# Retention layer: score products on 32-row parts of TensorE, queries masked for four heads at once, value bias added by GpSimd

## The chip, the cores and the metric

One core of one Trainium2 chip runs the program. The metric is the device time in microseconds (us). The kernel before takes 3194.3 us, the median of three runs (3193.05 to 3195.33). All numbers are float32.

## The reference, cut to what matters

The program is a chain of twelve layers on 2048 tokens of 128 features (2 batches of 1024). Only one layer is changed, the second, which the kernel calls `retention`. It gets the normalised x and its result is added to x:

```python
qkv = x @ W_qkv.T + b_qkv
q, k, v = jnp.split(qkv, 3, axis=-1)
# 16 heads of 8 features each
q = _apply_rope(q, cos, sin)
k = _apply_rope(k, cos, sin)
scores = jnp.einsum('bhtd,bhsd->bhts', q, k)
mask = jnp.tril(jnp.ones((length, length), dtype=x.dtype))
retention = scores * mask[None, None]
out = jnp.einsum('bhts,bhsd->bhtd', retention, v)
```

There is no softmax, so the product can be split: inside a tile of 128 tokens the masked scores are formed, and all earlier tiles enter through a running sum of k times v, the state.

## The kernel before, in words

Each layer is a block of its own with one program per engine; a barrier of all engines stands between two layers. In every block the order of the work on an engine is the order in which it is written, and semaphores tie the engines together. x, the weights and all intermediates stay in SBUF.

The retention block works on 16 tiles of 128 tokens, in 4 chunks of 4 tiles (`TPC` = 4). It has two parts.

The preparation goes chunk by chunk. TensorE turns the normalised rows (L268), ScalarE copies them to `xnT` (L1545), TensorE forms q and k and their rotated partners (L1458, L1460), then the values of four tiles (L1466), each with a second product of one row of ones by the bias row (L1468) into the same place, and turns the keys of the chunk before (L1444). VectorE applies the rotary tables (L1604, L1606, L1609) and the normalisation of the chunk ahead (L183, L186, L193). ScalarE copies the values and the turned keys out of PSUM (L1555, L1558). The tables come by four DMAs that SyncE issues at the start of the block (L1436); ScalarE and VectorE wait for all four.

The main loop goes in 16 waves, four per chunk. A wave is four heads on the four tiles of a chunk, so a wave has four steps, one for each tile. For a wave ScalarE makes four copies of the chunk's queries, each with all but one head's 8 features set to zero (`single_heads`, L1568). A step is one score product (L1482): 128 keys by 4 heads x 128 queries, contracted over all 128 features, of which the zeros leave 8. VectorE multiplies the 128x512 result by the triangle of ones (`mask`, L1616). Then four products (L1495) multiply the masked scores of each head by its 8 value columns; they go to four column groups of the array, 32 columns apart. TensorE issues step k+1's scores ahead of step k's values. Once per wave there is also one product of keys and values for the state (`outer`, L1504), which VectorE adds up (L1627 to L1632), and ScalarE copies the wave's values out of PSUM (L1580). After the first wave of each next chunk, TensorE puts the finished chunk together (`results`, L1517 and L1520: one product with the state and four that put the heads in place, for each tile), and VectorE adds it to x (L1638). In the waves 13 and 14 VectorE also does the first chunk's statistics and normalisation for the next layer.

PSUM has eight banks. The main loop gives the scores a ring of three, the state product one, the values two and the results two. A matmul in float32 appears in the trace as two weight loads and two matmuls, called two passes here.

Outside the block nothing is changed, except that the two constant tables `one_of` and `place` are filled in another way.

Of the kernel before, what the change touches and what calls it, by code (L numbers as in the profile page):

```python
# [25 lines left out]
P = 128  # L26
# [46 lines left out]
def macaron(nc, a, out):  # L73
    with ExitStack() as ctx:
# [1328 lines left out]
        def retention(tag, after):  # L1403
# [7 lines left out]
            qz = c(3 * GROUP * CHUNK).rearrange("p (n j t) -> p n j t", n=3, j=GROUP)  # L1411
            pr = c(8 * CHUNK).rearrange("p (n j t) -> p n j t", n=8, j=GROUP)
# [6 lines left out]
            HEADS = 4 * GROUP  # L1419
            one_of = c(HEADS + 1)  # L1420
            s = sems(tag, "tab stats rstd xn tp xT vec pool proj rope ktp ktc vps vcp qz st pm u sd "
                          "zero av oc y x")
            PER_BATCH = SEQ // P
            OUTER = 3
            OWN, SUM = (4, 5), (6, 7)

            STEPS = CHUNKS * GROUP * TPC
# [5 lines left out]
            def sync(sp):  # L1433
                for dst, name in ((tab, "r0_tab"), (blocks, "same"), (one_of, "one_of"),
                                  (place, "place")):
                    sp.dma_start(dst, a[name]).then_inc(s.tab, 16)  # L1436

            def tensor(pe):
# [10 lines left out]
                for ch in range(CHUNKS):  # L1449
# [24 lines left out]
                def own_scores(k):  # L1474

                    w, i = divmod(k, TPC)
                    n = w // GROUP * TPC + i
                    if i == 0:
                        pe.wait_ge(s.qz, w + 1)
                    if k >= 3:  # L1480
                        pe.wait_ge(s.pm, k - 2)
                    nc.tensor.matmul(ps[:, k % 3, :].rearrange("p (j t) -> p j t", j=GROUP),  # L1482
                                     kT[:, n * P:(n + 1) * P], qz[:, w % 3, :, i * P:(i + 1) * P],
                                     start=True, stop=True).then_inc(s.st, 1)

                def own_values(k):

                    w, i = divmod(k, TPC)
                    n, g = w // GROUP * TPC + i, w % GROUP
                    if i == 0 and w >= 2:  # L1490
                        pe.wait_ge(s.oc, w - 1)
                    pe.wait_ge(s.pm, k + 1)
                    for j in range(GROUP):
                        h = GROUP * g + j
                        last = nc.tensor.matmul(ps[32 * j:32 * j + 8, OWN[w % 2], i * P:(i + 1) * P],  # L1495
                                                vt[:, n, 8 * h:8 * h + 8], pr[:, k % 8, j, :],
                                                start=True, stop=True, tile_position=(0, 32 * j))
# [9 lines left out]
                def results(ch):  # L1507

                    pe.wait_ge(s.oc, GROUP * (ch + 1))
                    if ch >= 2:  # L1510
                        pe.wait_ge(s.x, ch - 1)
                    for n in range(ch * TPC, (ch + 1) * TPC):
                        at = ps[:, SUM[ch % 2], n % TPC * P:(n % TPC + 1) * P]
# [28 lines left out]
            def scalar(act):  # L1542
# [6 lines left out]
                act.wait_ge(s.tab, 64)  # L1549
# [11 lines left out]
                def single_heads(w):  # L1561
                    ch, g = divmod(w, GROUP)
                    act.wait_ge(s.rope, 2 * ch + 1)
                    if w >= 3:
                        act.wait_ge(s.st, TPC * (w - 2))
# [884 lines left out]
```

## Time and profile before

| | us |
|---|---|
| median of 3 runs | 3194.3 |
| the profiled execution | 3187.41 |
| its span, first to last instruction | 3185.7 |
| TensorE busy in the span | 2839.3 |
| VectorE busy | 2305.9 |
| ScalarE busy | 1871.4 |
| GpSimd busy | 511.1 |
| the retention block in the span | from about 221.1 to 380.8 |
| mean granted TensorE clock | 0.941 of full |

The profile is of one execution. Start times are us from the span's beginning. PE is TensorE's matmuls and PEld its weight loads, DVE is VectorE, ACT ScalarE, POOL GpSimd, SP SyncE. Matmuls are pipelined, so the time from one record's start to the next tells more than a record's own duration. A bracket at a row's end holds how long the engine was idle before it and what ended the wait.

### The profile page before, as it was taken

Reading aid. Unit: us, or ns where it says so; the run is one execution under the profiler, and the core shown is the slowest. Engines: PE = TensorE matmul, PEld = TensorE weight load, DVE = VectorE, ACT = ScalarE, POOL = GpSimd, SP = SyncE. Lnnn points to the kernel's source line nnn. Section 1 sums busy time; section 2 is a strip of 40 time slices with the busy share of each in tenths; the row PEclk is TensorE's granted clock in tenths of the full one; section 3 lists DMA queues with packets and bytes.
Section 4 is the critical chain, followed back from the end, with each engine's and each line's share of the span. In section 5 each row is a group of like instructions: output and inputs, shape, how many; then the busy total and the mean of one; then the engine's idle time right before and its main releaser. Section 6 shows DMA issues by size and latency. Waiting matters only on the chain. (4 is left out here: it accounts for less than half of the span.)

```text
span 3185.7 us, 43575 instructions
## 1 busy us (share of the span) xinstructions
PE 2839.3 (89%) x15916; PEld 1065.8 (33%) x15916; DVE 2305.9 (72%) x3016; ACT 1871.4 (59%) x3785; POOL 511.1 (16%) x832
## 2 busy tenths in 40 slices
PE   5999989799999998789977999999988799976778
PEld 2443434222222222533322222222226333344336
DVE  5464545799999996466657999999954766654972
ACT  2214322388888887446654888888875466654103
POOL 0000000200000000122222000000002222222740
PEclk9998999699999999989996999999999799988979
DMA  3210032300000000121113000000000311000000
GB/s 115 87 61 1 4 97 76 127 19 19 19 19 19 19 19 24 56 72 48 38 33 122 19 19 19 19 19 19 19 23 12 98 42 45 25 26 26 0 0 15
DMA packets 68129, 122.86 MB, mean 39 GB/s; under 512 B 16194, under 2 KB 43075, under 8 KB 64748
## 3 DMA queue, kind: packets, MB, share of 16 engines
q1 hardware_dynamic: 67916, 120.08, 11.6%
q8 instruction: 127, 2.08, 0.3%
q14 instruction: 86, 0.70, 0.1%
HBM read 96.56 MB, written 23.48 MB: 38 GB/s over the span
## 5 line engine op out<-in xcount | busy, mean ns | idle before, releaser
L1282 DVE TENSOR_REDUCE arena<-ps 128x1 f32<-128x1024 f32 (+7 forms) x1536 | 1572.6, 1064 | 235.8 <-PE ps L909 155.6
L1160 ACT ACTIVATE arena<-ps 128x512 f32<-128x512 f32 (+3 forms) x2816 | 1382.5, 573 | 410.1 <-PE ps L972 409.2
L903 PE MATMUL ps<-arena 61*128 61x512 bf16 (+4 forms) x2816 | 955.1, 384 | 65.5 <-DVE arena L1282 35.1
L972 PE MATMUL ps<-arena 64*128 64x512 bf16 (+4 forms) x2816 | 746.8, 372 | 56.0 <-ACT arena L1160 35.6
L929 PE MATMUL ps<-arena 128*32 128x512 f32 (+3 forms) x5632 | 713.6, 579 | 0.7 <-POOL arena L1241 0.3
L972 PEld LDWEIGHTS ps<-arena 64*128 64x128 bf16 (+1 forms) x2816 | 206.3, 95 | 767.2 <-ACT arena L1160 541.7
L903 PEld LDWEIGHTS ps<-arena 61*128 61x128 bf16 (+1 forms) x2816 | 259.5, 96 | 409.5 <-DVE arena L1282 354.9
L337 PE MATMUL ps<-xnT,moe_up 128*128 128x512 f32 x480 | 234.4, 614 | 0.0
L453 ACT ACTIVATE arena<-ps 128x512 f32<-128x512 f32 x120 | 71.4, 597 | 226.6 <-PE ps L337 226.6
L523 DVE TENSOR_TENSOR arena<-arena,ps 128x512 f32<-128x512 f32 x120 | 82.2, 686 | 160.8 <-ACT arena L453 129.8
L1210 POOL TENSOR_TENSOR arena<-arena,ones 16x128 bf16<-16x128 f32 x96 | 42.8, 446 | 844.1 <-ACT arena L1145 781.4
L929 PEld LDWEIGHTS ps<-arena 128*32 128x32 f32 x5632 | 111.3, 108 | 158.6 <-issue 135.4
L348 PE MATMUL ps<-arena,moe_dn 128*128 128x512 f32 x240 | 123.7, 607 | 17.4 <-DVE arena L533 15.2
L1241 POOL TENSOR_SCALAR_AFFINE_SELECT arena<-arena 128x512 f32<-128x512 f32 x128 | 81.2, 634 | 361.0 <-ACT arena L1160 359.2
L337 PEld LDWEIGHTS ps<-xnT,moe_up 128*128 128x128 f32 x480 | 92.7, 197 | 113.4 <-issue 109.0
L909 PE MATMUL ps<-maskb,identb 128*128 128x128 bf16 x512 | 115.4, 230 | 0.0
L253 POOL TENSOR_SCALAR var<-mv 128x4 f32<-128x4 f32 x40 | 9.6, 239 | 654.9 <-DVE mv L186 654.9
L2022 ACT ACTIVATE xnT<-ps,cols 128x512 f32<-128x512 f32 x8 | 6.2, 774 | 172.7 <-PE ps L268 172.7
L1342 DVE RECIPROCAL hid<-hid 128x512 f32<-128x512 f32 x16 | 53.5, 3346 | 52.5 <-DMA hid<-f_o 30.2
L1197 POOL TENSOR_TENSOR arena<-arena,ones 128x128 f32<-128x128 f32 (+1 forms) x48 | 22.5, 470 | 386.4 <-PE ps L929 386.4
L268 PE MATMUL ps<-ident,xn 128*128 128x128 f32 x208 | 36.6, 305 | 51.9 <-DVEq L203 27.0
L533 DVE TENSOR_TENSOR arena<-arena 128x512 f32<-128x512 f32 x120 | 80.9, 683 | 0.0
(226 smaller groups left out, 2640.3 us busy)
## 6 DMA issues: line engine op xcount, KB each, us to landing
arena<-m_w SPq DMA_DIRECT2D x32, 512.0 KB, 3.6
arena<-f_q SPq DMA_DIRECT2D x60, 144.0 KB
arena<-f_k SPq DMA_DIRECT2D x180, 48.0 KB
arena<-m_w SPq DMA_DIRECT2D x64, 128.0 KB, 3.7
arena<-in_w SPq DMA_DIRECT2D x4, 2048.0 KB
arena<-a_q SPq DMA_DIRECT2D x14, 576.0 KB
arena<-a_k SPq DMA_DIRECT2D x42, 192.0 KB
a_q<-arena SPq DMA_DIRECT2D x44, 96.0 KB, 2.0
```

Of the source, the lines that this page charges most:

```text
L337: nc.tensor.matmul(ps[:, FIRST_UP + tile % RING, :], moe_up[:, w:w + P], xnT[:, ch * CHUNK:(ch + 1) * CHUNK], start=True, stop=True)\
L348: nc.tensor.matmul(ps[:, Y_BANK, :], moe_dn[:, i * D:(i + 1) * D], hid[:, n % HID_RING, :], start=i == 0, stop=i == ALL_HID - 1)\
L453: nc.scalar.activation(sg[:, n % 3, :], ps[:, FIRST_UP + (2 * n) % RING, :], ACT.Silu).then_inc(s.silu, 1)
L523: nc.vector.tensor_tensor(hid[:, n % HID_RING, :], sg[:, n % 3, :], ps[:, FIRST_UP + (2 * n + 1) % RING, :], ALU.mult)\
L533: nc.vector.tensor_tensor(hid[:, n % HID_RING, :], hid[:, n % HID_RING, :], wb[:, 3 * p if last_pair else i, :], ALU.mult)\
L903: last = nc.tensor.matmul(at[:, k0 // CHUNK, 0:n], score_rows(Qop[par], j, slice(q0, q0 + P)), score_rows(Kop[par], j, slice(k0, k0 + n)), ...
L909: last = nc.tensor.matmul(at[:, (width - 1) // CHUNK, off:off + P], identb[:, :], maskb[:, 0, :], start=False, stop=True)
L929: last = nc.tensor.matmul(ps[32 * j:32 * j + 32, O_BANK, off:CHUNK], vx[vpar][:, kb, j, :], pr[:, (at % 2) * 4 + j, off:CHUNK], start=kb = ...
L972: nc.tensor.matmul(ps[:, ring_bank(item), off:CHUNK], shifted_rows(Kop[par], j, slice(kb * P, (kb + 1) * P)), shifted_rows(Qop[par], j, sl ...
L1160: nc.scalar.activation(pr[:, (at % 2) * 4 + j, off:CHUNK], ps[:, ring_bank(item), off:CHUNK], ACT.Exp).then_inc(s.ex, 1)
L1241: nc.gpsimd.affine_select(block, block, [[0, GROUP], [1, P]], ALU.is_ge, zero_fill, base=0, channel_multiplier=-1).then_inc(s.tri, 1)
L1282: nc.vector.tensor_reduce(mq[:, half, j * 4 + qb:j * 4 + qb + 1], src, AXX, ALU.max).then_inc(s.sread, 1)
```

## The change

- The heads are grouped in another way: a wave takes one head out of each group of 32 features (heads m, 4+m, 8+m, 12+m, where it took four neighbours).
- One ScalarE instruction per wave zeroes all but 8 of each 32 features, so that `qz` holds one 128x512 copy per wave instead of four; `one_of` shrinks from 17 to 5 columns.
- The score product of a head and a tile is contracted over the 32 features of its group alone: 16 products of 32 rows, 128 keys and 128 queries per wave, instead of 4 of 128 rows, 128 keys and 512 queries. They go to four banks, one per head. Heads 0 and 1 (row groups 0 and 32) are issued in turn over the four tiles, then heads 2 and 3.
- The order is by waves: all scores of wave w+1, then all values of wave w. A mask takes one head's four tiles; its count and its size stay.
- The results have one bank instead of two, the state product has bank 7.
- The bias products are gone. The bias row is sent to all 128 partitions by a fifth DMA at the block's start, and GpSimd adds it to the values in SBUF, one 128x512 addition per chunk.

```diff
-            qz = c(3 * GROUP * CHUNK).rearrange("p (n j t) -> p n j t", n=3, j=GROUP)
-            pr = c(8 * CHUNK).rearrange("p (n j t) -> p n j t", n=8, j=GROUP)
+            qz = c(3 * CHUNK).rearrange("p (n t) -> p n t", n=3)
+            pr = c(8 * CHUNK).rearrange("p (n i t) -> p n i t", n=8, i=TPC)
+            vbias = c(D)
...
-            OUTER = 3
-            OWN, SUM = (4, 5), (6, 7)
+            OWN, SUM, OUTER = (4, 5), 6, 7
+            WAVES = CHUNKS * GROUP
...
+                sp.dma_start(vbias, a["rows"][0:1, 9 * D:10 * D].to_broadcast([P, D])).then_inc(s.tab, 16)
...
-                        nc.tensor.matmul(at, xnT[:, ch * CHUNK + n * P:ch * CHUNK + (n + 1) * P],
-                                         wp[:, 2, :], start=True, stop=False)
-                        last = nc.tensor.matmul(at, ones[0:1, :], row(9), start=False, stop=True)
+                        last = nc.tensor.matmul(at, xnT[:, ch * CHUNK + n * P:ch * CHUNK + (n + 1) * P],
+                                                wp[:, 2, :], start=True, stop=True)
...
+                def own_scores(w, side):
+                    ch = w // GROUP
+                    if side == 0:
                         pe.wait_ge(s.qz, w + 1)
+                    if w:
+                        pe.wait_ge(s.pm, GROUP * (w - 1) + 2 * side + 2)
+                    for i in range(TPC):
+                        t = slice(ch * CHUNK + i * P, ch * CHUNK + (i + 1) * P)
+                        for j in (2 * side, 2 * side + 1):
+                            r = slice(32 * j, 32 * j + 32)
+                            last = nc.tensor.matmul(ps[:, j, i * P:(i + 1) * P], kT[r, t],
+                                                    qz[r, w % 3, i * P:(i + 1) * P],
+                                                    start=True, stop=True, tile_position=(32 * j, 0))
+                    last.then_inc(s.st, 1)
+                def own_values(w):
+                    ch, m = divmod(w, GROUP)
+                    if w >= 2:
                         pe.wait_ge(s.oc, w - 1)
+                    pe.wait_ge(s.pm, GROUP * (w + 1))
+                    for i in range(TPC):
+                        for j in range(GROUP):
+                            h = GROUP * j + m
+                            last = nc.tensor.matmul(ps[32 * j:32 * j + 8, OWN[w % 2], i * P:(i + 1) * P],
+                                                    vt[:, ch * TPC + i, 8 * h:8 * h + 8],
+                                                    pr[:, w % 2 * GROUP + j, i, :],
+                                                    start=True, stop=True, tile_position=(0, 32 * j))
                     last.then_inc(s.av, 1)
...
-                pe.wait_ge(s.vcp, CHUNKS)
+                pe.wait_ge(s.vb, CHUNKS)
...
-                own_scores(0)
+                own_scores(0, 0)
+                own_scores(0, 1)
                 pe.wait_ge(s.zero, 1)
-                for w in range(CHUNKS * GROUP):
+                for w in range(WAVES):
                     outer(w)
-                    for k in range(w * TPC, (w + 1) * TPC):
-                        if k + 1 < STEPS:
-                            own_scores(k + 1)
-                        own_values(k)
+                    if w + 1 < WAVES:
+                        own_scores(w + 1, 0)
+                        own_scores(w + 1, 1)
+                    own_values(w)
...
+                    nc.scalar.activation(qz[:, w % 3, :], qT[:, ch * CHUNK:(ch + 1) * CHUNK], ACT.Identity,
+                                         bias=one_of[:, GROUP:GROUP + 1],
+                                         scale=one_of[:, m:m + 1]).then_inc(s.qz, 1)
...
+                for ch in range(CHUNKS):
+                    tiles = vt[:, ch * TPC:(ch + 1) * TPC, :]
+                    pool.wait_ge(s.vcp, ch + 1)
+                    nc.gpsimd.tensor_tensor(tiles, tiles, vbias.unsqueeze(1).to_broadcast([P, TPC, D]),
+                                            ALU.add).then_inc(s.vb, 1)
```

## Rows read from the trace of the kernel before

**Rows 1.** Windows: preparation, main loop; wall, busy of each engine (records), clock, DMA.
```profile
218.00:265.60 47.60, 37.69 (x133) 21.13 (x132) 24.91 (x62) 10.14 (x18) 3.78 (x6) 0.85 0.09 30
265.60:380.80 115.20, 112.60 (x824) 48.13 (x824) 55.62 (x106) 51.64 (x76) 1.26 (x2) 0.97 0.00 1
```

**Rows 2.** Timeline of a wave: start us, us, engine, line, operation.
```profile
275.02 0.30 PEld L1504 LDWEIGHTS ps<-arena 128*128 128x128 f32 x2 [0.22 <-issue]
...
276.63 0.30 PEld L1482 LDWEIGHTS ps<-arena 128*128 128x128 f32 x2 [0.22 <-issue]
...
277.69 0.12 PEld L1495 LDWEIGHTS ps<-arena 128*8 128x8 f32 x8 [0.76 <-DVE arena L1616]
...
278.02 0.30 PEld L1482 LDWEIGHTS ps<-arena 128*128 128x128 f32 x2 [0.22 <-issue]
...
280.81 0.30 PEld L1504 LDWEIGHTS ps<-arena 128*128 128x128 f32 x2 [0.22 <-issue]
```

**Rows 3.** Timeline, the results of chunk 0.
```profile
298.17 0.97 PEld L1520 LDWEIGHTS ps<-arena 128*128 128x128 f32 x8 [0.22 <-issue]
...
301.29 0.30 PEld L1517 LDWEIGHTS ps<-arena 128*128 128x128 f32 x2
...
302.41 0.30 PEld L1504 LDWEIGHTS ps<-arena 128*128 128x128 f32 x2
```

**Rows 4.** Timeline, values and bias of chunk 1, then the turned keys of chunk 0.
```profile
235.66 0.19 PEld L1466 LDWEIGHTS ps<-wproj,xnT 128*128 128x128 f32 x1 [0.24 <-issue]
...
238.05 0.30 PEld L1466 LDWEIGHTS ps<-wproj,xnT 128*128 128x128 f32 x2
...
238.88 0.42 PEld L1444 LDWEIGHTS ps<-ident,arena 128*128 128x128 f32 x4
```

**Rows 5.** Timeline of layer f1: 64-row and 61-row products; float32 loads in 32-column groups.
```profile
900.34 0.16 PEld L929 LDWEIGHTS ps<-arena 128*32 128x32 f32 x8 [0.23 <-issue]
...
901.34 0.39 PE L972 MATMUL ps<-arena 64*128 64x512 bf16 x1
901.35 0.39 PE L903 MATMUL ps<-arena 61*128 61x512 bf16 x1
901.57 0.38 PE L972 MATMUL ps<-arena 64*128 64x512 bf16 x2
```

**Rows 6.** Timeline, VectorE: the block's start, and late in the loop.
```profile
227.01 0.75 DVE L1604 SCALAR_TENSOR_TENSOR arena<-ps,cols,arena 128x512 f32<-128x512 f32 x1 [1.76 <-DMA arena<-in_place]
...
233.44 0.42 PEld L268 LDWEIGHTS ps<-ident,xn 128*128 128x128 f32 x4 [0.70 <-DVE xn L193]
...
363.37 0.68 DVE L1638 TENSOR_TENSOR x<-x,ps 128x512 f32<-128x512 f32 x1
...
365.66 1.28 DVE L1616 TENSOR_TENSOR arena<-ps,masks 128x512 f32<-128x512 f32 x2
```

**Rows 7.** Timeline: chunk 3's last rotation, the first queries, the loop's first and last instructions.
```profile
258.39 0.69 DVE L1609 TENSOR_TENSOR arena<-arena 128x512 f32<-128x512 f32 x1
...
262.57 2.92 ACT L1568 ACTIVATE arena<-arena 128x512 f32<-128x512 f32 x4
...
265.60 0.50 PEld L1482 LDWEIGHTS ps<-arena 128*128 128x128 f32 x2 [3.96 <-issue]
...
375.32 0.30 PEld L1517 LDWEIGHTS ps<-arena 128*128 128x128 f32 x2 [1.00 <-ACT arena L1580]
```

**Rows 8.** Groups: durations (min/median/max ns), first and last start.
```profile
L1632 DVE TENSOR_TENSOR arena<-arena x12: 291/292/293, 275.9 to 365.4; 128x128 f32<-128x128 f32 x12
L1192 POOL TENSOR_TENSOR arena<-arena x32: 1147/1153/1173, 578.5 to 2526.7; 128x512 bf16<-128x512 f32 x32
```

**Rows 9.** Windows, columns as in Rows 1: the clock beside the bias products, and early in the loop.
```profile
229.00:240.00 11.00, 10.54 (x46) 6.38 (x44) 9.55 (x26) 1.02 (x2) 1.27 (x2) 1.00 0.01 2
266.00:270.00 4.00, 4.00 (x14) 1.33 (x13) 1.03 (x3) 4.00 (x7) 0.00 (x0) 0.50 0.01 4
```

**Rows 10.** Timeline, twelve small products in the first layer.
```profile
58.71 0.91 PE L375 MATMUL ps<-ident,arena 9*128 9x9 f32 x12
```

More of the change, by code:

```diff
@@ L1472, in tensor @@
                 turn_keys(CHUNKS - 1)
[L1474 to L1478, printed above, removed]
+                def own_scores(w, side):
+                    ch = w // GROUP
+                    if side == 0:
                         pe.wait_ge(s.qz, w + 1)
[L1480 to L1490, printed above, removed]
-                        pe.wait_ge(s.oc, w - 1)
[L1492 to L1497, printed above, removed]
+                    if w:
+                        pe.wait_ge(s.pm, GROUP * (w - 1) + 2 * side + 2)
@@ L1509, in results @@
                     pe.wait_ge(s.oc, GROUP * (ch + 1))
[L1510 to L1511 removed]
+                    if ch:
+                        pe.wait_ge(s.x, ch)
                     for n in range(ch * TPC, (ch + 1) * TPC):
[L1513 removed]
+                        at = ps[:, SUM, n % TPC * P:(n % TPC + 1) * P]
                         first = n % PER_BATCH == 0
@@ L1559, in scalar, with quarter @@
                                          ACT.Copy).then_inc(s.ktc, 1)
-                def single_heads(w):
-                    ch, g = divmod(w, GROUP)
+                def quarter(w):
+                    ch, m = divmod(w, GROUP)
                     act.wait_ge(s.rope, 2 * ch + 1)
                     if w >= 3:
-                        act.wait_ge(s.st, TPC * (w - 2))
-                    for j in range(GROUP):
-                        h = GROUP * g + j
-                        last = nc.scalar.activation(qz[:, w % 3, j, :],
-                                                    qT[:, ch * CHUNK:(ch + 1) * CHUNK], ACT.Identity,
-                                                    bias=one_of[:, HEADS:HEADS + 1],
-                                                    scale=one_of[:, h:h + 1])
-                    last.then_inc(s.qz, 1)
+                        act.wait_ge(s.st, 2 * (w - 2))
+                    nc.scalar.activation(qz[:, w % 3, :], qT[:, ch * CHUNK:(ch + 1) * CHUNK], ACT.Identity,
+                                         bias=one_of[:, GROUP:GROUP + 1],
+                                         scale=one_of[:, m:m + 1]).then_inc(s.qz, 1)
                 for w in range(3):
-                    single_heads(w)
+                    quarter(w)
                 for w in range(CHUNKS * GROUP):
-                    act.wait_ge(s.av, TPC * (w + 1))
+                    act.wait_ge(s.av, w + 1)
                     if w >= 2 * GROUP:
@@ L1581, in scalar @@
                         .then_inc(s.oc, 1)
-                    if w + 3 < CHUNKS * GROUP:
-                        single_heads(w + 3)
+                    if w + 3 < WAVES:
+                        quarter(w + 3)
             def gpsimd(pool):
@@ L1610, in vector, with mask @@
                             .then_inc(s.rope, 1)
-                def mask(k):
-                    dve.wait_ge(s.st, k + 1)
-                    if k >= 8:
-                        dve.wait_ge(s.av, k - 7)
+                def mask(w, j):
+                    dve.wait_ge(s.st, 2 * w + j // 2 + 1)
+                    if w >= 2 and j == 0:
+                        dve.wait_ge(s.av, w - 1)
                     nc.vector.tensor_tensor(
-                        pr[:, k % 8], ps[:, k % 3, :].rearrange("p (j t) -> p j t", j=GROUP),
-                        masks[:, 2, :].unsqueeze(1).to_broadcast([P, GROUP, P]), ALU.mult)\
+                        pr[:, w % 2 * GROUP + j], ps[:, j, :].rearrange("p (i t) -> p i t", i=TPC),
+                        masks[:, 2, :].unsqueeze(1).to_broadcast([P, TPC, P]), ALU.mult)\
                         .then_inc(s.pm, 1)
@@ L1642, in vector @@
                 nc.vector.memset(ps[:, OWN[0]:OWN[1] + 1, :], 0.0).then_inc(s.zero, 1)
-                mask(0)
-                for w in range(CHUNKS * GROUP):
+                for j in range(GROUP):
+                    mask(0, j)
+                for w in range(WAVES):
                     next_state(w)
-                    for k in range(w * TPC, (w + 1) * TPC):
-                        if k + 1 < STEPS:
-                            mask(k + 1)
+                    if w + 1 < WAVES:
+                        for j in range(GROUP):
+                            mask(w + 1, j)
                     if w % GROUP == 1 and w > 1:
```

16 lines of the change are left out of this document (7 added, 9 removed).

## The prediction

> **What bounds the kernel now.** The layers are cut apart by barriers, so I read only the retention block, first by windows. In the main loop (265.6 to 380.8) TensorE is busy 112.6 of 115.2 us, VectorE 55.6, ScalarE 51.6 [rows 1]. So TensorE sets the pace. The timeline says with what. One step runs from 276.63 to 278.02, 1.39 us [rows 2]. From the scores' first load to the values' first load it is 1.06 us (277.69 - 276.63), then 0.33 us of values. In dense products of the same type a tile of ten passes over 128 columns takes 1.12 us (302.41 - 301.29), 0.11 us a pass [rows 3], so 512 columns are about 0.43 us a pass and the two passes of a score product 0.85. The rest of 1.06, some 0.2 us, is a first load that nothing hides, and the emptying of the array before the shape of its parts changes; the same stands in the 0.33, as two passes of 128 columns are 0.22 and the four column groups run side by side. A wave takes 5.79 us (275.02 to 280.81), of which 5.79 - 4 x 1.39 = 0.23 is the state product [rows 2].
>
> The preparation (to 265.6) is a chain of TensorE, ScalarE and back [rows 4], with two places where VectorE or a DMA comes last [rows 6].
>
> **The main loop, part by part.** Scores: 16 products a wave, 32 passes of 128 columns, as many columns as before. What can go is the half of them that lies beside the other half. No row shows 32-row products in float32. The nearest are the 64- and 61-row products of layer f1, in bfloat16: a pair on different row groups starts within 0.01 us, and the next starts 0.22 us later [rows 5], so two products take the time of one. That float32 loads of several parts overlap too is seen in column groups: eight loads of 32 columns take 0.16 us, where two of 128, as many columns, take 0.30 [rows 2, 5]. Bounds: full overlap, 16 passes of 0.11 = 1.78 us; none, 3.56 us. I take full overlap. With a first load (0.11) and one emptying (0.1): 2.0 us.
>
> The page "TensorE: Matmul & The Clock Gate" of the Trainium skill (LDWEIGHTS) says that a load's time goes by its columns, not its rows, and (The mechanism) that a load passes a running matmul only on another row group. By this each part would alternate load and product, and two parts would give 3.5 us a wave instead of 1.8. In this trace loads on the same rows do hide: 0.11 us a pass with a new 128-column load each [rows 3].
>
> Values: 16 products a wave in four column groups, so 8 passes of 0.11 = 0.89, plus 0.1 of emptying: 1.0 us (4 x 0.33 = 1.32 before) [rows 2]. State product: it now stands between two changes of shape. Exactly this is in the bias stretch, where value products of two passes take turns with one-row products: one of each takes 0.83 us (238.88 - 238.05), 0.41 apiece [rows 4]. Sum: 0.41 + 2.0 + 1.0 = 3.4 us a wave instead of 5.79, 2.4 us less.
>
> Does VectorE keep up? Four masks back to back are 4 x 0.62 (two in 1.28 us, [rows 6]) and the state 0.29 for each of its two instructions plus a small gap [rows 8]: 3.1 us, under 3.4. Worked through in order from the start of the state product: S0 (heads 0, 1) ends at 1.4, masks from 1.5 to 4.0; S1 of the next wave starts at 3.4 + 1.4 = 4.8 and needs the last mask, 0.8 us of slack; the next state update ends at 4.7, when the next masks may start (4.9). So TensorE still leads, with 0.2 us to spare. ScalarE, busy 51.6 us of the loop before [rows 1], loses three of four query masks, so it stays hidden. The single results bank waits for an addition three waves old, hidden.
>
> At the end it isn't hidden: in wave 13 the addition (0.68) and the statistics (in all from 363.37 to the masks at 365.66, with a state update of 0.6 in it) [rows 6] stand ahead of wave 15's masks, so 1.7 us plus a wait for them. With 3.1 of 3.4 us used, wave 15's values come 2.4 us late.
>
> Loop: before, 375.32 - 265.60 = 109.7 us to the last results [rows 7]. After: first scores 1.9; half clock at the start as before (0.50 in 266 to 270, [rows 9]; with its edges I take 5.5 us of TensorE work at half speed), 2.8; 15 waves of 3.4 = 51; three in-loop results as before, 4.24 each (302.41 - 298.17, [rows 3]) = 12.7; last values 1.0; the late masks 2.4; ScalarE's copy 0.8. Sum 72.6, so **37 us less**. The last results are unchanged.
>
> **The preparation.** Values of a chunk take 238.88 - 235.66 = 3.22 us, eight turns of 0.41 [rows 4]; without the bias products 8 passes of 0.11 and one first load, 1.0 us: 2.2 us less for each chunk. What follows hangs on it (the turned keys, L1444 [rows 4], their copy L1558, the copy L1545, then the next projection). Chunk 0's gain is lost: TensorE next waits for VectorE's normalised rows at 233.44, whose chain starts at 227.01 when the last table lands [rows 6]. That chain starts later, too: the fifth DMA is issued behind the fourth, which I put at +0.45. Bounds: 0, if it lands with the others, and 1.8, the wait for the fourth once more [rows 6]; the value taken is nearer to the first, as transfers in flight overlap. Chunks 1 and 2 give 4.4. In chunk 3 the values gain 2.2, but turning the last keys needs VectorE's last rotation, which ends at 258.39 + 0.69 = 259.08, some 6 us ahead of the loop [rows 7]. Between it and the loop stand the last turned keys, their copy and the query mask, so a part of the 2.2 is lost behind it; the older chunk's keys are turned first and fill the wait. I count 1.9, with 0 and 2.2 as its bounds. The first queries: four instructions of 2.92 us in all become one of 0.80, 2.2 less [rows 7]. GpSimd's last addition is near 1.15 us (the L1192 row, same size, [rows 8]) behind the value copy; key turning, key copy and query mask behind the same copy take longer (the mask alone is 2.92 / 4 = 0.73, [rows 7], and a key copy of the same size stands before it), so it hides. Were it 3 us it would cost 1. Sum 4.4 + 1.9 + 2.2 - 0.45 = **8 us less**.
>
> Total 45 us. The profiled execution took 3187.4, 6.9 us below the median of the runs; taken from the median, 3194.3 - 45 = **3149.3 us**.
>
> **Rivals.**
>
> A: the score parts don't overlap, because the 128-column loads go one after another or because float32 pairs run in turn. For: no float32 row groups in the trace. Against: both halves of it appear separately [rows 5]. A wave is 0.41 + 3.8 + 1.0 = 5.2 us, 0.6 less; VectorE has room again, so no late end: 16 x 0.6 = 9, plus 8 from the preparation: 17 to 19 us less, 3176.
>
> B, slower: TensorE can't be fed. A wave has 132 loads and matmuls. At 3.4 us this is 51 ns for each pair of load and matmul; before, 42 pairs in 5.79 us, 138 ns. The densest longer run of pairs that I find is of twelve in 0.91 us, at most 76 ns each [rows 10], and they may have been queued ahead; over a longer stretch none is denser than the results' 111 ns [rows 3]. At 76 ns a wave is 66 x 0.076 = 5.0 us, 26 us of the gain gone: 3175. Half of that is 3162. At 111 ns it is 7.3: the loop 1.5 x 16 = 24 us longer, less 8, so 3210. It decides above (5.79 + 0.5)/66 = 95 ns. Against: the eight loads of the values all lie within 0.12 us [rows 2]. The same page of the Trainium skill (section "Wait — 56ns, not 53.3ns?") gives some 62 ns for each matmul where it is decoded in software: by it alone a wave would be 66 x 0.062 = 4.1 us, an estimate, and the time 3160.
>
> C, slower: the granted clock stays at half (1.2 GHz) in the loop, as half the rows work. Passes double: a wave 6.5, results 8.5: so the loop is 16 x 0.7 + 4 x 4.3 = 28 us longer, less 8: 3214. Against: in the bias stretch, half of whose products had one row, the clock was 1.00 [rows 9]. It was at half in the loop's first us, behind 3.96 us without a load [rows 7, 9], and this pause gets shorter.
>
> D: VectorE leads because masks slow down beside TensorE's writes to four banks or beside GpSimd. At 3.8 us a wave: 3156. This is a shade of the forecast.
>
> **How the numbers follow.** Forecast with D and a small part of B: 0.72, own range 3141 to 3163. A, or B up to 76 ns: 0.17. B beyond 95 ns: 0.05. C: 0.03. The rest, 0.03, ends near no change. A measurement of this kernel can tell 0.2%, 6.4 us, from none. Faster 0.89, same 0.03, slower 0.08. The range reaches from 3140 (all passes overlap, clock drops vanish) to 3178 so as to hold A.
>
> **What would show it.** Right: in the changed trace two score matmuls on different row groups start together, the time between state products is 3.3 to 3.6 us with TensorE without gaps; masks come in fours, 0.62 us apart; the preparation is some 8 us shorter; the last masks are late behind the statistics. Wrong: score matmuls 0.11 us apart one by one (A), gaps between loads while all waits are met (B), 0.50 in the clock column (C), TensorE idle before scores until a mask (D).

## The result, and the profile after

| | before | after |
|---|---|---|
| median, us | 3193.68 (4 runs, 3189.15 to 3195.33) | 3140.53 (4 runs, 3137.83 to 3144.41) |
| ratio, 95% interval | | 0.9839, 0.9824 to 0.9854 |
| the profiled execution / its span | 3187.41 / 3185.7 | 3137.83 / 3136.1 |
| retention block, barrier to barrier | 160.5 | 114.1 |
| the other eleven layers together | 3025.2 | 3022.0 |

The kernel is 53 us faster; the forecast was 45 less. The measured 3140.5 lies at the lower edge of what was forecast: 0.5 us under the range of 3141 to 3163 that had the chance of 0.72, and 0.5 above the lower end of the whole range, 3140 to 3178. In the profiled executions 46.4 us of the 49.6 come from the changed block. The other 3 come from layers in which no work changed. There the clock stood at half for 355 us before and for 338 after; over all the kernels below the sum over these layers went from 3016.2 us, with 331 at half clock, to 3030.8, with 372. These stretches fall otherwise in every execution. So the block's own length, barrier to barrier, is the sharper measure, and I use it beside the medians.

The block has three parts. From its first instruction to the loop's first score load: 265.60 - 221.34 = 44.26 before, 251.53 - 219.42 = 32.11 after, 12.1 less (forecast 8). From there to the last results: 109.7 before, 324.16 - 251.53 = 72.6 after, 37.1 less (forecast 37). The last results, to the end of the last addition: 5.5 before, 331.80 + 0.69 - 324.16 = 8.3 after, 2.9 more (forecast: nothing).

Windows of the kernel after: the preparation, the loop's first stretch, the middle of the loop, the stretch behind the last values (columns as in [rows 1]).

```profile
218.00:251.50 33.50, 24.19 (x96) 13.54 (x96) 24.67 (x62) 7.40 (x14) 8.85 (x10) 0.95 0.13 44
251.70:265.20 13.50, 13.50 (x160) 11.28 (x164) 8.02 (x15) 2.43 (x4) 0.00 (x0) 0.50 0.00 1
265.60:298.00 32.40, 32.14 (x570) 28.74 (x568) 21.42 (x42) 10.39 (x16) 0.00 (x0) 1.00 0.01 2
323.40:330.20 6.80, 6.09 (x32) 6.04 (x29) 0.00 (x0) 0.60 (x1) 0.00 (x0) 0.50 0.01 2
```

In the middle TensorE is busy 32.14 of 32.40 us at the full clock: it leads, as forecast. But the loop's first 13.5 us and the block's last results stand at 0.50, and busy is 13.50 of 13.50: no window of busy time would show that this half is lost.

The timeline of one wave after, which answers to [rows 2]:

```profile
271.79 0.49 PE L1507 MATMUL ps<-arena 128*128 128x128 f32 x2
272.21 1.53 PEld L1483 LDWEIGHTS ps<-arena 32*128 32x128 f32 x32
273.42 1.89 DVE L1621 TENSOR_TENSOR arena<-ps,masks 128x512 f32<-128x512 f32 x3 [0.18 <-PE ps L1483]
273.86 0.77 PEld L1497 LDWEIGHTS ps<-arena 128*8 128x8 f32 x32
274.85 0.52 PEld L1523 LDWEIGHTS ps<-arena 128*128 128x128 f32 x4 [0.22 <-issue]
```

State product 272.21 - 271.79 = 0.42 us, scores 273.86 - 272.21 = 1.65, values 274.85 - 273.86 = 0.99: 3.06 us for a wave of 66 load and matmul pairs, 46 ns a pair. VectorE waits 0.18 us for the scores. In a wave with an addition of results VectorE's work is longer, and it is VectorE that leads: the scores took 305.15 - 303.05 = 2.10, the wave 306.14 - 302.63 = 3.51.

```profile
302.63 0.49 PE L1507 MATMUL ps<-arena 128*128 128x128 f32 x2
303.05 1.99 PEld L1483 LDWEIGHTS ps<-arena 32*128 32x128 f32 x32
305.15 0.77 PEld L1497 LDWEIGHTS ps<-arena 128*8 128x8 f32 x32
306.14 0.30 PEld L1507 LDWEIGHTS ps<-arena 128*128 128x128 f32 x2 [0.22 <-issue]
```

The starts of single records in the first of these two waves show how 32 passes fit into 1.65 us, where 16 pairs of passes one after another, 0.11 each, would make 1.76 and a first load more:

```
row groups  0, 32: first passes start 272.212, 272.218; the next pair 0.21 later, then one every 0.11; last 273.095, 273.102
row groups 64, 96: first passes start 272.772, 272.779; the next pair 0.21 later, then one every 0.11; last 273.656, 273.662
```

The records don't name their row group; they are told apart by these steps. So the second pair of row groups, later in the program's order, began 0.32 us before the first pair had started its last pass, and for that time all four row groups work side by side.

The loop's start and end, TensorE's records:

```profile
251.56 3.00 PE L1483 MATMUL ps<-arena 32*128 32x128 f32 x32 [1.48 <-ACT arena L1570]
254.50 0.80 PE L1507 MATMUL ps<-arena 128*128 128x128 f32 x2
260.08 0.80 PE L1507 MATMUL ps<-arena 128*128 128x128 f32 x2
265.55 0.49 PE L1507 MATMUL ps<-arena 128*128 128x128 f32 x2
...
322.39 1.06 PE L1497 MATMUL ps<-arena 128*8 128x128 f32 x32 [2.63 <-DVE arena L1621]
324.16 0.50 PEld L1520 LDWEIGHTS ps<-arena 128*128 128x128 f32 x2 [1.00 <-ACT arena L1580]
...
331.80 0.69 DVE L1643 TENSOR_TENSOR x<-x,ps 128x512 f32<-128x512 f32 x1 [8.53 <-PE ps L1523]
```

Waves 0 and 1 take 5.58 and 5.47 us, not 3.06. At the end wave 15's values wait 2.63 us for the last mask.

### The profile page after: what moved, and what is told of

It is laid out like the page before. It is cut to its first block and busy times, and to the rows that moved or that the text cites. A ratio compares the mean times of both kernels' runs of the same rounds, so it can differ in the third digit from the quotient of the medians.

```text
span 3136.1 us, 44146 instructions
## 1 busy us (share of the span) xinstructions
PE 2777.3 (89%) x16220; PEld 1074.6 (34%) x16268; DVE 2302.1 (73%) x3016; ACT 1838.0 (59%) x3737; POOL 516.5 (16%) x836
## 5 line engine op out<-in xcount | busy, mean ns | idle before, releaser
L972 PE MATMUL ps<-arena 64*128 64x512 bf16 (+4 forms) x2768 | 735.0, 371 | 67.1 <-ACT arena L1160 39.8
```

The lines of the kernel that those rows point to most:

```text
L972: nc.tensor.matmul(ps[:, ring_bank(item), off:CHUNK], shifted_rows(Kop[par], j, slice(kb * P, (kb + 1) * P)), shifted_rows(Qop[par], j, sl ...
```

## The experiments

All kernels but one are the changed kernel with the tables `one_of` and `place` sent as in the kernel before and put in their new order by GpSimd on the chip. The first run is this control. Behind "Measured" stand the median, then its ratio to the kernel before, which ran beside it on the same chip. The block times, and the "half clock", which are the stretches of 0.50 in TensorE's clock column inside the block, are of the one profiled execution.

**Control.**

```diff
-    o["one_of"] = (feat[:, None] % 32 // hd == np.arange(GROUP + 1)[None, :])
+    o["one_of"] = (feat[:, None] // hd == np.arange(17)[None, :])
...
+                nc.gpsimd.tensor_tensor(one_of, pairs[:, 0:GROUP], pairs[:, GROUP:2 * GROUP], ALU.add)
```

> The changed kernel, with the two constant tables sent as before and put in the new order by GpSimd in the preparation (two additions of 16 and 8 columns, four copies of 128x128). It is the base of the experiments that follow. GpSimd idles there until the first value copy, so every theory expects the changed kernel's time: a median within 3 us of 3140.5, a wave of 3.1 to 3.2 us, and a retention block of 114 us.

Measured: 3141.44, ratio 0.9853 (0.9837 to 0.9869); block 114.4 us; half clock 3.41 us at 222.16, 13.65 from 252.88 and 6.83 from 324.56. It stands for the changed kernel.

**What the row groups are worth: the same order, all 128 rows in each product.**

```diff
-  nc.tensor.matmul(ps[:, j, i * P:(i + 1) * P], kT[r, t], qz[r, ...], tile_position=(32 * j, 0))
+  nc.tensor.matmul(ps[:, j, i * P:(i + 1) * P], kT[:, t], qz[:, ...])
```

> Each score product is contracted over all 128 rows instead of its 32, so it sums over the four heads of the wave and the output is another one; the number of products, their columns, the order by waves and all waits stay. It takes away the overlap alone. Theory (overlap): 32 passes of 0.11 in a row, scores 3.5 us, state product 0.21 (no change of shape behind it), values 1.0 and 0.1 for one change of shape: a wave of 4.9 us, 16 x 1.7 = 27 us slower than the base, 3167; so of the loop's gain of 2.6 us a wave, 1.7 is the overlap and 0.9 the order by waves. Rival (the order by waves is all): the wave stays at 3.1 and the time with it. Rival (narrow products cost clock): the half-clock stretch at the loop's start, 13.65 us in the changed kernel and 10.24 before, gets shorter.

Measured: 3164.74, ratio 0.9927 (0.9912 to 0.9942); block 133.9. Timeline of a wave, and a window over 10 us early in the loop:

```profile
268.98 0.49 PE L1510 MATMUL ps<-arena 128*128 128x128 f32 x2
269.20 3.65 PEld L1486 LDWEIGHTS ps<-arena 128*128 128x128 f32 x32
272.97 0.77 PEld L1500 LDWEIGHTS ps<-arena 128*8 128x8 f32 x32
273.96 0.30 PEld L1510 LDWEIGHTS ps<-arena 128*128 128x128 f32 x2 [0.22 <-issue]
...
257.50:267.70 10.20, 10.20 (x115) 9.86 (x115) 7.23 (x13) 1.30 (x2) 0.00 (x0) 1.00 0.01 2
```

The scores take 3.77 us, the wave 4.98. So the row groups bring 4.98 - 3.06 = 1.9 us a wave, and the new order alone 5.79 - 4.98 = 0.8. I put the 0.8 down to fewer changes of shape and fewer uncovered first loads; no run takes these apart. Rival A of the prediction had 3.8 us of scores and a wave of 5.2 without overlap; it is 3.77 and 4.98. The expectation's last rival holds as well: the half clock at the loop's start is gone, and so is that at the end. This is why the block lost only 133.9 - 114.4 = 19.5 us against the control and not 16 x 1.9 = 30: TensorE worked 6.8 us at half clock here and 23.2 in the control (8.2 us of time), and there is no wait of 2.6 us for the last masks.

**Does the overlap need the groups issued in turn?**

```diff
-                    for i in range(TPC):
-                        for j in (2 * side, 2 * side + 1):
+                    for j in (2 * side, 2 * side + 1):
+                        for i in range(TPC):
```

> The same 16 score products per wave, but one row group's four tiles one after another, then the next group's. Theory (the gain is the overlap of row groups, and it hangs on the order of issue, because TensorE looks only a few records ahead): products on one row group can't overlap, and the next group starts at most some three passes early, as the second pair did in the changed kernel (272.77, when the first pair had 0.33 us left). Scores 4 x 0.86 - 3 x 0.33 = 2.5 us instead of 1.65, a wave of 3.9 (3.5 to 4.3), 12 us slower than the base (6 to 18). Rival (the order is free, TensorE's window holds all of a wave): no change. Rival (the gain is the order by waves, with fewer changes of the array's shape): no change.

Measured: 3166.38, ratio 0.9931 (0.9916 to 0.9945); block 139.8. TensorE's timeline of a wave at the full clock, then two windows at half and one at full clock:

```profile
306.62 2.82 PE L1486 MATMUL ps<-arena 32*128 32x128 f32 x32
309.37 1.06 PE L1500 MATMUL ps<-arena 128*8 128x128 f32 x32
...
262.00:278.00 16.00, 16.00 (x142) 13.58 (x141) 6.47 (x13) 2.59 (x4) 0.00 (x0) 0.50 0.00 1
278.00:298.00 20.00, 20.00 (x181) 16.59 (x181) 8.76 (x16) 3.62 (x6) 0.00 (x0) 0.50 0.00 1
299.00:320.00 21.00, 21.00 (x307) 19.29 (x306) 11.89 (x22) 5.19 (x8) 0.00 (x0) 1.00 0.01 3
```

The scores take 2.75 us: TensorE does begin a later row group early, but only near the end of the earlier one (the records show the next group's first pass 0.33 us before the last of the group before). The overlap takes 3.77 - 2.75 = 1.0 us off a wave's scores, where pairs take 2.1 off. And the clock stays at half for 41 us, with TensorE busy without a gap in the windows shown, then goes to full in the same kind of work. So the kernel is 25 us slower than the control, where 6 to 18 were expected: the overlap's part was seen rightly, the clock's wasn't.

**All four row groups in turn.** One wait, for all masks of the wave before, ahead of all 16 products.

```diff
-                        for j in (2 * side, 2 * side + 1):
+                        for j in range(GROUP):
```

> All four row groups are issued in turn, as one group of 16 products that waits for all four masks of the wave before. Theory (all four row groups can run beside each other, and VectorE's four masks and the state update, 3.1 us, now set the wave): scores take 0.11 + 8 x 0.107 = 0.97 us instead of 1.65, but the time is worse, since VectorE now idles from its last mask to the end of the next scores: 2.48 of masks + 1.1 to 1.2 of scores and hand-over = 3.6 to 3.7 us a wave instead of 3.1 to 3.2, 8 us slower than the base. Rival (only two row groups run beside each other): scores stay at 1.65 or more, a wave of 4.2 us or more, 16 us slower. Rival (TensorE sets the wave and four groups make it shorter): a wave of 2.5, 9 us faster.

Measured: 3145.74, ratio 0.9868 (0.9851 to 0.9884); block 118.5. Timeline of a wave:

```profile
268.44 1.01 PEld L1488 LDWEIGHTS ps<-arena 32*128 32x128 f32 x32 [0.60 <-issue]
269.58 0.77 PEld L1502 LDWEIGHTS ps<-arena 128*8 128x8 f32 x32
269.71 2.48 DVE L1639 TENSOR_TENSOR arena<-ps,masks 128x512 f32<-128x512 f32 x4 [0.85 <-PE ps L1488]
272.31 0.34 PEld L1488 LDWEIGHTS ps<-arena 32*128 32x128 f32 x8 [1.44 <-ACT arena L1578]
272.34 0.39 PE L1488 MATMUL ps<-arena 32*128 32x128 f32 x4 [1.28 <-DVE arena L1639]
```

Scores in 1.14 us: four groups overlap too. But now nothing of a wave's masks lies beside its scores, TensorE idles 1.28 us for the last mask, and the wave takes 272.31 - 268.44 = 3.87: VectorE's 3.1 us of work and its wait of 0.85 for the scores stand one behind the other. Pairs are the better order. The block is 4.1 us longer than the control's; 8 were expected. The page "TensorEngine Tiling (Array Packing)" of the Trainium skill (PSUM Bottleneck) says that emptying PSUM may become the bottleneck once tiling makes TensorE faster; by the row above, it has: 2.48 us of masks and 0.6 of state updates to 2.55 us of TensorE's work.

**The value bias alone**, on the kernel before: fifth DMA, bias products out, GpSimd's addition in.

> The kernel before with one part of the change alone: no bias products, the bias row by a fifth DMA, added by GpSimd. Theory of the prediction's sum: 2.2 us less for chunks 1 and 2, 1.9 for chunk 3, 0.1 more for the fifth DMA: 6.2 us less at the same clock. The two half-clock stretches of the preparation (3.4 us each, at 240.7 and 251.0 in the kernel before) were absent in the changed kernel; if this part alone removes them it gives another 3 us, 9 in all. Rival (the preparation's gain was clock alone, and TensorE would have waited anyway): 3 us or less.

Measured: 3178.61, ratio 0.9955 (0.9938 to 0.9972); block 151.2, 9.3 less than before. TensorE's timeline: of the kernel before, behind the bias stretches, then the same places of this kernel.

```profile
238.47 0.48 PE L1468 MATMUL ps<-rows,ones 1*128 1x128 f32 x2
240.71 2.08 PE L1458 MATMUL ps<-xnT,wproj 128*128 128x512 f32 x2 [1.17 <-ACT xnT L1545]
...
251.43 2.08 PE L1458 MATMUL ps<-xnT,wproj 128*128 128x512 f32 x2 [1.18 <-ACT xnT L1545]
```

```profile
233.23 1.11 PE L268 MATMUL ps<-ident,xn 128*128 128x128 f32 x4 [2.20 <-DVE xn L193]
...
237.11 1.05 PE L1468 MATMUL ps<-wproj,xnT 128*128 128x128 f32 x8
239.77 1.12 PE L1460 MATMUL ps<-xnT,wproj 128*128 128x512 f32 x2 [1.18 <-ACT xnT L1546]
...
246.42 1.12 PE L1460 MATMUL ps<-xnT,wproj 128*128 128x512 f32 x2 [1.18 <-ACT xnT L1546]
...
257.20:260.50 3.30, 3.30 (x6) 1.10 (x4) 0.89 (x2) 3.30 (x6) 0.00 (x0) 0.50 0.00 0
```

Two passes of 512 columns take 1.12 us here and 2.08 before, behind a wait of 1.18 in both. Ahead of the wait, half of the value products had one row before; without them that stretch is also shorter, and no run takes the two apart. The half clock isn't gone from this kernel, though. A stretch of 3.41 us came at 233.23, behind a wait of 2.20 between products of 128 rows, and the one at the loop's start lasted 3.41 instead of 10.24. TensorE worked 16.4 us at half clock before and 10.2 here. That is 3.1 us of time, so 6.2 of the 9.3 are left at the same clock, the figure of the prediction's sum.

**The next layer's statistics behind the last masks.**

```diff
-                    if w == CHUNKS * GROUP - 3:
-                        ahead_stats(dve, s, t, CHUNKS, after)
-                    if w == CHUNKS * GROUP - 2:
-                        ahead_apply(dve, s, CHUNKS, after)
+                ahead_stats(dve, s, t, CHUNKS, after)
+                ahead_apply(dve, s, CHUNKS, after)
                 add(CHUNKS - 1)
```

> The base e0 with the next layer's statistics and normalisation moved behind VectorE's last masks, where VectorE idles 8.5 us. Theory (they hold up wave 15's masks: TensorE idles 2.6 us before the last values and the clock then falls for the last results, 2.9 us): block 5.5 us shorter, 3136. Without the clock's part 2.6. Rival (they hide, the last wave is late for another reason): no change.

Measured: 3139.96, ratio 0.9833 (0.9818 to 0.9847); block 111.8, 2.6 less than the control, where 5.5 were expected. TensorE's wait for the last mask fell from 2.63 to 1.46 us; that is this edit's doing. The half clock at the end fell from 6.83 to 3.41, but a stretch of 6.83 came at 333.59, in the next layer, which took 188.1 us where it had taken 185.5. This second part can't be put down to the edit: the control's own repeat, the last run below, has the same 3.41 at the end, another 6.83 in the next layer, and 188.0 us for it. The whole kernel gained nothing that can be told.

```profile
321.30 1.06 PE L1500 MATMUL ps<-arena 128*8 128x128 f32 x32 [1.46 <-DVE arena L1637]
```

**Two masks of 1024 columns instead of four of 512.**

```diff
-                        pr[:, w % 2 * GROUP + j], ps[:, j, :].rearrange("p (i t) -> p i t", i=TPC),
+                        pr[:, at:at + 2].rearrange("p n i t -> p (n i) t"),
+                        ps[:, 2 * side:2 * side + 2, :].rearrange("p j (i t) -> p (j i) t", i=TPC),
```

> The base e0 with the wide masks alone. If VectorE sets the wave where it has more than its four masks and the state update to do, the waves with an addition get shorter (3.1 to 3.2 instead of 3.2 to 3.5) and wave 15's values come 0.3 us earlier: 1 to 2 us in the block, 112 to 113 instead of 114.4. The half-clock stretch of 13.65 us at the loop's start stays, as the pause stays. Rival (masks don't matter): 114.4. Rival (a mask of two banks waits longer for its scores and delays the chain): 115 or more.

Measured: 3142.44, ratio 0.9846 (0.9829 to 0.9864); block 112.1, 2.3 less than the control. The pair takes 2.36 us where four take 2.48. Of the 2.3 us, 1.7 are a half-clock stretch of 3.41 instead of 6.83 at the end, which the control's repeat has as well (block 112.8). So 0.6 to 0.7 us may be the masks' own; by medians nothing is gained.

```profile
270.00 2.36 DVE L1638 TENSOR_TENSOR arena<-ps,masks 128x1024 f32<-128x1024 f32 x2 [0.18 <-PE ps L1486]
```

**What sets the clock at the loop's start?** In the kernel after, TensorE pauses 1.48 us (1.68 without a load) ahead of the first scores and then does 32-row products. Either could be the cause. One kernel keeps the pause and gives waves 0 and 1 all 128 rows:

```diff
+                            if w < 2:
+                                last = nc.tensor.matmul(ps[:, j, i * P:(i + 1) * P], kT[:, t],
+                                                        qz[:, w % 3, i * P:(i + 1) * P], ...)
+                                continue
```

> The base e0, but the score products of waves 0 and 1 are contracted over all 128 rows, as in the third experiment, so their output is another one; the pause before the loop stays. Theory N (narrow products let the clock stay at half after a pause; with all rows it had no half-clock stretch in the loop): no half-clock stretch at the loop's start, or one of 3.4 us at most. Theory P (the pause alone makes it, and the third experiment was luck): a stretch of 10 us or more as in the base. The two waves cost 1.9 us more each at full clock.

Measured in one execution: 3140.17; block 112.3. TensorE's timeline and the window:

```profile
254.69 3.81 PE L1487 MATMUL ps<-arena 128*128 128x128 f32 x32 [1.48 <-ACT arena L1581]
263.63 1.72 PE L1491 MATMUL ps<-arena 32*128 32x128 f32 x32
...
251.00:264.00 13.00, 10.29 (x113) 9.38 (x113) 7.99 (x14) 4.44 (x8) 1.26 (x1) 1.00 0.01 1
```

The pause is there, the half clock isn't, and the narrow products that follow run at full clock. Two waves of twice the passes cost no more than the half clock did.

The other kernel keeps the narrow products and takes the pause away: scores of wave 0 ahead of the last turned keys, query masks as soon as a chunk's queries are there; it has the late statistics as well.

```diff
-                turn_keys(CHUNKS - 1)
...
                 own_scores(0, 0)
+                pe.wait_ge(s.rope, 2 * CHUNKS)
                 own_scores(0, 1)
+                turn_keys(CHUNKS - 1)
```

> The kernel of the seventh experiment without the wide masks: early first scores and the late normalisation, four 128x512 masks a wave. If the pause before the loop is one of two conditions of the half clock there (the other being narrow products), the loop has no half-clock stretch, as in the seventh, and the block takes 102 + 2 = 104 us. If the seventh experiment's full clock was luck or came from the masks, the stretch of 10 to 14 us is back and the block takes 109 or more.

Measured: 3140.05, ratio 0.9837 (0.9817 to 0.9857); block 104.6. Timeline and window at the loop's start:

```profile
251.90 2.46 PE L1485 MATMUL ps<-arena 32*128 32x128 f32 x32
255.63 0.49 PE L1509 MATMUL ps<-arena 128*128 128x128 f32 x2 [0.69 <-ACT arena L1579]
258.80 0.49 PE L1509 MATMUL ps<-arena 128*128 128x128 f32 x2
...
250.00:262.00 12.00, 11.17 (x183) 9.24 (x182) 11.11 (x20) 2.98 (x5) 1.27 (x1) 1.00 0.00 1
```

Wave 0 takes 3.17 us at once. So the half clock at the loop's start goes with both together: a pause of 1.48 us and then narrow products. With both it came in all seven profiled executions that have them: for 13.65 us in four (after, the control, the late statistics alone, the wide masks alone), for 10.24 in two (the control's repeat, and the four row groups in turn, where it began only in a second pause of 2.27), for 41 in the one with the groups one after another. With the pause and 128 rows it came in neither of two (the third experiment's way and this section's first kernel), with narrow products and no such pause in none of three (this kernel and the last one, twice). The block gained 9.8 us over the control, or 7.2 over the kernel with the late statistics alone, yet the medians are level. In its profile the other layers took 3030.8 us, with 372 at half clock; the control's 3019.9, with 335. Whether that is this kernel's doing or chance, one profile of each can't say.

**All three together**, and again with five executions, beside the control on the same chip.

> e5 with two more edits: the first scores are issued ahead of the last turned keys, their query masks made by ScalarE while it idles in the preparation, so that TensorE idles no more than some 0.5 us there; and VectorE masks two heads' scores with one 128x1024 instruction, two a wave instead of four. Early scores: 1.5 to 2 us, and, if the half-clock stretch of 13.65 us at the loop's start comes from the pause before it, 5 us more; if it comes from the narrow products, nothing more. Wide masks: VectorE's 3.1 us a wave fall by 2 x 0.09 to 2.9, under TensorE's 3.06, worth 0.1 to 0.2 a wave in the waves with an addition and at the end, 1 to 2 us in all. Sum: 3 to 4 us under e5 with the half clock, 8 to 9 without.

Measured: 3130.55 (3119.93 to 3136.82), ratio 0.9802 (0.9779 to 0.9825); block 102.0, 2.6 less than without the wide masks. Of these 1.7 are a half-clock stretch of 3.41 us at 233.72 that only the other has.

> The kernel of e7_wide_masks again (early first scores, wide masks, late normalisation), with the base beside it on one chip. Its retention block took 102.0 us and the base's 114.4, while the other layers of single executions differ by up to 15 us in sum. If the block's gain is real in the whole kernel's time, the median is 9 to 13 us under the base's; if the other layers give it back, under 5.

Measured: 3131.21 (3127.38 to 3149.87), ratio 0.9819 (0.9794 to 0.9844); block 102.1; half clock only 3.41 us at 220.41.

> The base e0 again, beside the last kernel on one chip: 3137 to 3145 us, a retention block of 114 us with a half-clock stretch of 10 to 14 us at the loop's start, if that stretch belongs to the kernel and not to one execution.

Measured: 3139.78 (3138.34 to 3143.24), ratio 0.9838 (0.9824 to 0.9851); block 112.8; half clock 3.41 at 223.88 and 234.12, 10.24 at 254.60, 3.41 at 326.28.

The three together have the shortest block: 10.7 to 12.4 us under the control's. The medians are 8.6 us under it on one chip, just short of the 9 to 13 expected if the whole gain stays, and 10.9 in the first pair, which ran on two chips. The intervals of the last two ratios still overlap a little (0.9844 and 0.9824), so from the repeat alone the order of the two isn't proven; with the block times it is the likelier reading. In the first of the two profiles, the window over the end of the loop and the last results shows the clock at full throughout (the next half-clock stretch, 6.83 us, comes at 323.47 in the next layer):

```profile
300.00:320.50 20.50, 17.71 (x284) 15.93 (x280) 11.61 (x24) 3.09 (x5) 1.26 (x2) 1.00 0.01 2
```

## Why the prediction was right, and where only by luck

The steps of the block, by kernels: before 160.5; bias to GpSimd 151.2; order by waves and one query mask a wave 133.9; row groups 114.4; pause, late statistics and wide masks 102.0.

**The loop**: forecast 72.6 us, measured 72.6. The sum is right, its terms are not, and that it comes out is luck: the first scores and the waves were put 5.4 us too high, the half clock, the results, the last wait and the waves that VectorE leads 5.4 too low.

| term | forecast | measured |
|---|---|---|
| first scores, at full clock | 1.9 | 1.65 |
| 15 waves | 51 (3.4 each) | 45.9 (3.06 each) |
| waves in which VectorE leads | none | about 1.0 (the remainder of the sum) |
| lost to the half clock | 2.8 | 6.8 (13.65 / 2) |
| three results in the loop | 12.7 | 12.9 (4.24, 4.46, 4.24) |
| wait for wave 15's masks | 2.4 | 2.6 |
| last values, ScalarE's copy | 1.8 | 1.8 (324.16 - 322.39) |

- *Scores 2.0 us a wave*: 1.65. Full overlap within a pair was right; that the next pair overlaps the end of this one was missed. I took from the results' passes [rows 3] that a load on the same rows hides behind the running product, against what the page "TensorE: Matmul & The Clock Gate" of the Trainium skill (The mechanism) says of loads, that they overlap with a running product only on another row group. It held: a pair every 0.11 us, each pass with a new load.
- *State 0.41, values 1.0*: 0.42 and 0.99. The price of a change of shape, read in the bias stretch [rows 4], carried over exactly.
- *"TensorE still leads, with 0.2 us to spare"*: true in plain waves (VectorE waits 0.18), at 3.06 and not 3.4. Since TensorE became faster than forecast, the spare went where an addition stands (3.51).
- *"Half clock at the start as before", 2.8*: this step failed. I took the cost as before, and against rival C that it shrinks with the pause. The pause did shrink, from 3.59 us to 1.48, but the half clock lasted 13.65 us, where 5.8 of its 10.24 us had lain in the loop before.

**The preparation**: forecast 8, measured 12.1; the clock makes 3.2 of the difference. TensorE's timeline after, where it starts on each chunk:

```profile
231.65 0.66 PE L268 MATMUL ps<-ident,xn 128*128 128x128 f32 x4 [2.20 <-DVE xn L193]
236.53 1.12 PE L1457 MATMUL ps<-xnT,wproj 128*128 128x512 f32 x2 [1.18 <-ACT xnT L1549]
243.17 1.12 PE L1457 MATMUL ps<-xnT,wproj 128*128 128x512 f32 x2 [1.18 <-ACT xnT L1549]
```

- *Chunk 0's gain is lost*: yes. From the block's first instruction to this load 12.10 us before, 12.23 after; the fifth DMA cost 0.13, not 0.45.
- *Chunk 1, 2.2*: 7.27 (240.71 - 233.44) became 4.88, 2.4 less.
- *Chunk 2, 2.2*: 10.72 (251.43 - 240.71) became 6.64, 4.1 less, of which 1.7 is the half clock that stood at 240.7 for 3.41 us.
- *Chunk 3 and the first queries, 1.9 + 2.2*: 14.17 (265.60 - 251.43) became 251.53 - 243.17 = 8.36, 5.8 less, of which 1.5 is the half clock (at 250.97, behind a wait again). That leaves 4.3, near the 4.1 forecast.
- *GpSimd's addition near 1.15 us, hidden*: 1.26 us, hidden. The last runs beside the turned keys:

```profile
249.40 1.26 POOL L1592 TENSOR_TENSOR arena<-arena 128x512 f32<-128x512 f32 x1 [4.45 <-ACT arena L1559]
249.43 0.66 PE L1443 MATMUL ps<-ident,arena 128*128 128x128 f32 x4 [1.23 <-DVE arena L1614]
```

The failed part is the clock. I wrote that in the bias stretch, half of whose products had one row, the clock was 1.00 [rows 9], and took that against rival C. The window ended at 240.00. The drop came at 240.72, behind that stretch and a pause of 1.17: the row that I needed was the next one.

**"The last results are unchanged"** failed, by 2.9 us: behind the wait for the late masks, which I had forecast rightly at 2.4, the clock stood at half for 6.83 us. The term was priced as idle time alone. Such a stretch came behind that wait in all six profiled executions in which it was 2.50 to 2.63 us, for 3.41 or 6.83; where the wait was 1.10 to 1.46, in one of five.

**The rivals.** A (no overlap) fell: 4.98 us a wave without it, 3.06 with it. B (TensorE can't be fed) fell: 46 ns a pair over a wave, denser than the 76 that I had for the densest run. C was half right: with narrow work the clock did stand at half, in the loop too, for 13.65 us in this kernel and for 41 in the one with the groups one after another, but only behind a pause and not in the whole loop. D (masks slower beside other work) fell: four masks in 2.48 us, as before.

**What stays open.** Whether a pause brings the clock down isn't settled by the program alone. In the 13 profiled executions without bias products TensorE waits 2.20 us in the preparation, between products of 128 rows. A stretch of 3.41 came behind that wait in seven of them and none in six, and the control and its repeat, one program, are on different sides. So the seven, two and three executions above are few. Why the clock went back to full after 13.65 us in one order and 41 in the other, in steady work, no run separates. Nor does any run tell whether the late masks' pause needs narrow products before it to bring the clock down.

## What to carry to other kernels

Small contractions are worth putting side by side on row groups, if they are issued alternately (here each row group had its own bank; no run shares one); then look at once at the engine that empties PSUM, since it leads next. Price a pause of TensorE not by its idle time alone but with the clock behind it, and read the clock column beyond the end of the stretch that you judge. Fill the pause ahead of a stretch of narrow products (here by moving the first scores ahead of the last turned keys): it brought 7.2 us of block time, more than any mask or order of statistics, though alone it didn't show in the median.

## What the runs showed of the hardware that was not expected

- The granted clock fell to half (1.2 GHz) where a pause of 1.2 to 1.5 us met products of few rows (one row ahead of it in the preparation, 32 rows behind it in the loop). Behind it, it stayed there for 3.41 us in the preparation and for 13.65 and 41 in the loop, with TensorE busy all the time. Pauses of 1.2 to 1.5 us with 128-row products around them left the clock at full. Longer ones between such products didn't always: half clock came behind 2.20 us in seven executions of 13, and for 3.41 us at the loop's start of the bias kernel, behind 3.59.
- A row group's products start ahead of earlier ones on another row group: 0.32 us before the last start of the pair before. So a part of the overlap comes without alternation: 2.75 us for the scores one group after another, 3.77 with all rows, 1.65 in pairs, 1.14 in fours.
- 66 pairs of float32 load and matmul in 3.06 us, 46 ns a pair, sustained. The page "TensorE: Matmul & The Clock Gate" of the Trainium skill (Wait — 56ns, not 53.3ns?) gives some 62 ns for each matmul where it is decoded in software, by which a wave would be 4.1 us, an estimate. The measured 3.06 shows that this is no bound here; which way the matmuls were decoded, no run shows.
